# Keys and values of three context tiles made before the experts and kept in DRAM, in a two-layer perceiver kernel

## What is computed

```python
x = x + L0_xattn(layernorm(x), ctx_1024)      # 16 heads of 64
x = x + L0_attn(layernorm(x))                 # latent attention with rope ("mla")
x = x + L0_ffn(layernorm(x))                  # attention, then top-2 of 8 experts
x = x + L1_xattn(layernorm(x), ctx_1024, mask)# 16 heads of 16: the second cross-attention
x = x + L1_attn(layernorm(x))                 # causal attention
x = x + L1_ffn(layernorm(x))                  # weights of +1 and -1
# of L1_xattn, what matters here:
q = (query @ Wq + bq); k = (key @ Wk + bk); v = (value @ Wv + bv)
attn = softmax(where(mask == 0, -inf, q k^T * 16**-0.5));  out = (attn v) @ Wo + bo
```

## Time and profile before

| | us |
|---|---|
| median of 3 runs | 1094.91 |
| lowest, highest | 1089.47, 1100.26 |
| run that was profiled | 1091.17 |
| its span, first to last instruction | 1089.4 |

### The profile page before, as it was taken

The page is one execution under the profiler, slowest core; times in us unless marked ns, Lnnn a source line. Parts: engine busy times, 40 slices in busy tenths (PEclk is TensorE's granted clock), DMA queues, the critical chain, the costliest instruction groups (busy, mean ns, idle before and its releaser), DMA issues.

```text
span 1089.4 us, 27524 instructions
## 1 busy us (share of the span) xinstructions
PE 1025.6 (94%) x11715; PEld 883.0 (81%) x11715; DVE 640.2 (59%) x1376; ACT 472.3 (43%) x866; POOL 242.8 (22%) x381
## 2 busy tenths in 40 slices
PE   5999999999999899999399999997999998999998
PEld 4788888888888678887399999995888877887887
DVE  5745645545333455775659999976577652355342
ACT  3333333333333755643156677751534332464231
POOL 2311211211111124343414343414201000011000
PEclk9999999999999999997589999997999997999999
DMA  9300000000000800220226577613110001000000
GB/s 312 106 17 20 10 12 20 2 1 1 2 1 2 339 2 3 79 99 12 69 60 233 193 235 277 214 31 96 41 41 22 3 2 59 13 2 2 1 20 19
DMA packets 55672, 72.79 MB, mean 67 GB/s; under 512 B 8504, under 2 KB 48896, under 8 KB 54912
## 3 DMA queue, kind: packets, MB, share of 16 engines
q1 hardware_dynamic: 54016, 66.85, 18.4%
q0 software_dynamic: 1536, 4.20, 1.2%
HBM read 60.02 MB, written 11.01 MB: 65 GB/s over the span
## 4 chain that ended last, share of the span: by engine, by line
PE 84%; DVE 7%; ACT 3%; issue 3%; POOL 2%; DMA 1%; DVEq 0%; POOLq 0%; ACTq 0%
PE ps L615 8%; PE ps L630 8%; PE ps L2171 7%; PE ps L2187 7%; PE ps L2527 5%; PE ps L1469 4%; PE ps L599 3%; PE ps L1117 3%; PE ps L647 3%; PE ps L1387 3%; PE ps L667 3%; PE ps L569 3%; PE ps L1486 2%; PE ps L1426 2%; PE ps L1052 2%
## 5 line engine op out<-in xcount | busy, mean ns | idle before, releaser
L371 POOL TENSOR_TENSOR rn_tmp<-rn_cur,eps 128x1 f32<-128x1 f32 x48 | 14.6, 304 | 432.1 <-DVE rn_cur L365 432.0
L750 ACT ACTIVATE x0pT<-ps 128x512 f32<-128x512 f32 x64 | 38.3, 598 | 123.7 <-PE ps L630 123.7
L2171 PE MATMUL ps<-moe_xT_hi,ew_1hi 128*128 128x256 f32 x240 | 69.8, 291 | 2.3 <-DVE moe_xT_lo L2317 2.3
L2187 PE MATMUL ps<-ew_2hi,eh_hi 128*128 128x256 f32 x240 | 69.4, 289 | 2.4 <-DVE eh_lo L2325 2.4
L2323 DVE CAST eh_hi<-eh 128x512 fp32r<-128x512 f32 x60 | 63.4, 1056 | 13.9 <-ACT eh L2233 13.9
L2171 PE MATMUL ps<-moe_xT_lo,ew_1hi 128*128 128x256 f32 x240 | 68.9, 287 | 0.0
L2171 PE MATMUL ps<-moe_xT_hi,ew_1lo 128*128 128x256 f32 x240 | 68.8, 287 | 0.0
L2187 PE MATMUL ps<-ew_2hi,eh_lo 128*128 128x256 f32 x240 | 67.1, 279 | 0.0
L2187 PE MATMUL ps<-ew_2lo,eh_hi 128*128 128x256 f32 x240 | 66.9, 279 | 0.0
L857 DVE TENSOR_TENSOR x0A_lo<-ps,x0A_hi 128x512 fp32r<-128x512 f32 x64 | 41.0, 685 | 35.6 <-ACT x0A_hi L741 35.6
L2527 PE MATMUL ps<-f,ffw 128*128 128x512 f32 x256 | 59.2, 391 | 0.2 <-DVE f L2500 0.2
(11 more groups left out here) (330 smaller groups left out, 2832.1 us busy)
## 6 DMA issues: line engine op xcount, KB each, us to landing
ew<-L_ffn_W_dram SPq DMA_DIRECT2D x30, 1024.0 KB, 7.2
x0cin<-ctx_dram SPq DMA_DIRECT2D x8, 512.0 KB, 4.1
x1cin<-ctx_dram SPq DMA_DIRECT2D x8, 512.0 KB, 4.4
xg<-moe_in SPq DMA_DIRECT2D x15, 256.0 KB, 7.7
moe_out<-moe_y SPq DMA_DIRECT2D x15, 256.0 KB, 7.8
moe_in<-padneg SPq DMA_DIRECT2D x3, 1024.0 KB, 13.2
maskrow<-mask_BxS_ik_dram SPq DMA_DIRECT2D x2, 1024.0 KB, 7.7
x0wk<-L_xattn_Wkv_dram SPq DMA_DIRECT2D x1, 1024.0 KB, 7.1
```

The lines of the kernel that those rows point to most:

```text
L750: nc.scalar.activation(g.pT[:, u, :], ps[:, S_BANK[u % 2], :], ACT.Exp, scale=64.0 ** -0.5).then_inc(C0.exp, 1)
L2171: last = nc.tensor.matmul(ps[:, n % 3, j * BT:j * BT + BT], w[b % 2][:, i, f * P:f * P + P], v[b % 2][:, i, :], start=(i == 0 and m == 0), ...
L2187: last = nc.tensor.matmul(ps[:, O_BANK[b % 2] + c, 0:D], v[n % 3][:, j * BT + c * P:j * BT + c * P + P], w[b % 2][:, f, :], start=(f == 0 ...
```

## The change

With `EARLY` = 3, the K/V work of context tiles 0, 1 and 2 moves out of the second cross-attention.

- It is made in iterations 13 to 18 of the self-attention loop, between the pieces of the last items, on PE, ACT and DVE (`x1_cT`, `x1_k`, `x1_v`). Its buffers (`XE`) lie where the second expert's split weights and other late buffers stand, so the loads of those buffers and some splits come later.
- SP stores each finished tile (keys and values, 8.7 KB in each of 128 partitions, 1.1 MB) to the DRAM tensor `kv_early`, two buffers for three tiles, and loads all six parts again in and after the last expert block, into five buffers for keys and five for values.
- The split of the K/V weights is made twice, the first time in items 8 and 9, in place of two splits of expert 1, which move into expert block 0 (ACT, DVE and POOL one each for the parts 2 and 3).
- `weights_of(3)` moves behind `rows_of(2)`, into block 0. The load of `w_sq[1]` (1 MB) moves from the start of the kernel to block 5.
- In the second cross-attention tile 3's K/V work stands at the head, and the remaining four tiles are spread over the seven steps by `KV_STEP`: steps 0, 2, 4 hold a tile's `cT` and `k`, steps 1, 3, 5 its `v`, step 6 all of the last tile.
- `pool_x1` gathers two tiles before the first `rstd` where it gathered four; the others follow one for each norm.

```diff
+        EARLY = 3
...
+        class XE:
+
+            cin = nc.alloc_sbuf_tensor_at("xe_cin", [P, 2, 4, D], F32, offset=expert_at(1))
+            w_hi, w_lo = (nc.alloc_sbuf_tensor_at("xe_w_" + n, [P, KD, 2, D], F32R, offset=w_sq_at + 4 * KD * 4 * D + 4 * KD * 2 * D * i) for i, n in enumerate(("hi", "lo")))
+            cT_hi, cT_lo = (nc.alloc_sbuf_tensor_at("xe_cT_" + n, [P, KD, 512], F32R, offset=expert_at(7) + 4 * KD * 512 * i) for i, n in enumerate(("hi", "lo")))
+            kv = [nc.alloc_sbuf_tensor_at(f"xe_kv{i}", [P, KV_WORDS], F32, offset=expert_at(11) + 4 * KV_WORDS * i) for i in range(2)]
+            kT = [k[:, 0:KD * 512].rearrange("p (k n) -> p k n", k=KD) for k in kv]
...
+        KV_STEP = ((4, "k"), (4, "v"), (5, "k"), (5, "v"), (6, "k"), (6, "v"), (7, "kv"))
...
+        def wait_stored(eng, t):
+
+            if 1 < t < EARLY:
+                eng.wait_ge(C1.early_stored[t - 2], 16)
+
+        def wait_all_stored(eng):
+            for t in range(EARLY):
+                eng.wait_ge(C1.early_stored[t], 16)
+
...
-                fill_k(0, 0)
-                fill_k(0, 1)
-                fill_v(0, 0)
-                fill_v(0, 1)
+                fill_k(EARLY, 0)
+                fill_k(EARLY, 1)
+                fill_v(EARLY, 0)
+                fill_v(EARLY, 1)
                 fill_lat(0)
                 fill_q(0)
                 for t in range(T - 1):
                     old = t > 0
+                    j, part = KV_STEP[t]
                     scores(t, 0)
                     if old:
                         fill_pv(t - 1, 0)
-                    fill_cT(t + 1, 0)
-                    fill_cT(t + 1, 1)
+                    if part == "v":
+                        fill_v(j, 0)
+                    else:
+                        fill_cT(j, 0)
+                        fill_cT(j, 1)
                     if old:
                         fill_pv(t - 1, 1)
                     scores(t, 1)
                     if old:
                         fill_T(t - 1)
                     fill_lat(t + 1)
-                    fill_k(t + 1, 0)
+                    if part == "v":
+                        fill_v(j, 1)
+                    else:
+                        fill_k(j, 0)
                     if old:
                         fill_y(t - 1)
                     fill_neg(t, 1)
                     exponents(t, 0)
-                    fill_k(t + 1, 1)
+                    if part != "v":
+                        fill_k(j, 1)
                     fill_q(t + 1)
                     exponents(t, 1)
-                    fill_v(t + 1, 0)
-                    fill_v(t + 1, 1)
+                    if part == "kv":
+                        fill_v(j, 0)
+                        fill_v(j, 1)
                 return scores, fill_pv, fill_neg, fill_T, exponents, fill_y
 
...
         def pool_x1(pool):
-            for t in range(4):
+            for t in range(2):
                 moe_collect(pool, t)
             for phase, t in X1_ROWS:
                 row_rstd(pool, t, X1_ROWS[phase, t] % 2, phase, X1_ROWS[phase, t])
-                if phase == "x1" and t + 4 < T:
-                    moe_collect(pool, t + 4)
+                if phase == "x1" and t + 2 < T:
...
+                if span == 0 and n >= hi - 3:
+                    i = n - hi + 3
+                    if ahead:
+                        scores(n + 1)
+                    if front:
+                        fill_qk(n + 2, "k")
+                    elif i == 1:
+                        x1_k(0, 0)
+                    elif i == 2:
+                        x1_v(0, 1)
+                    elif i == 3:
+                        x1_k(1, 0)
+                    if back:
+                        fill_pv(n - 1, 0)
+                    if front:
+                        fill_qk(n + 2, "q")
+                    elif i == 1:
+                        x1_k(0, 1)
+                    elif i == 3:
+                        x1_k(1, 1)
+                    if back:
+                        fill_pv(n - 1, 1)
+                    if routed(span, n - 3):
+                        fill_router(n - 3)
+                    if front:
+                        fill_v(n + 2)
+                    elif i == 1:
+                        x1_v(0, 0)
+                    elif i == 3:
+                        x1_v(1, 0)
+                    elif i == 4:
+                        x1_k(2, 0)
+                        x1_k(2, 1)
+                    elif i == 5:
+                        x1_v(2, 1)
+                    if back:
+                        fill_T(n - 1)
+                    if here:
+                        exponents(n)
+                    if back:
+                        fill_y(n - 1)
+                    if i in (0, 2):
+                        x1_cT(i // 2, 0)
+                        x1_cT(i // 2, 1)
+                    if routed(span, n - 2):
+                        fill_mT(n - 2)
+                    if i == 3:
+                        x1_v(1, 1)
+                    if routed(span, n - 3):
+                        fill_rank(n - 3)
+                    if i == 3:
+                        x1_cT(2, 0)
+                        x1_cT(2, 1)
+                    elif i == 4:
+                        x1_v(2, 0)
...
+                    x1_v(2)
+                if span == 0 and 2 <= n < 8:
                     expert_upper(act, (n - 2) // 4, (n - 2) % 4)
+                if span == 0 and n == 8:
+                    act.wait_ge(ld["xw"], 64)
+                    nc.scalar.activation(XE.w_hi[:, :, :, :], xw[:, :, 1:3, :], ACT.Copy).then_inc(C1.w_hi, 1)
...
+            elif b == 1 and i > 1:
+                R1.wait_filled(act, EARLY - 1, "v1")
...
+            wait_all_stored(dve)
...
-                if p == 0 and 0 < b < NB - 1:
+                if p == 0 and b < NB - 1:
                     expert_lower(dve, b + 1, 2)
...
-            for i, w in enumerate("QKVO"):
-                whole(w_sq[1][:, :, i, :], weight("L1_attn_W_" + w), ld["sq1"])
...
+            def early_part(t, part):
+                at_kv = KD * 512 * part
+                dst = X1.v[t][:, :, :, :].rearrange("p k h d -> p (k h d)") if part else X1.kT[t][:, :, :].rearrange("p k n -> p (k n)")
+                sp.dma_start(dst, kv_dram[P * t:P * t + P, at_kv:at_kv + (KV_WORDS - KD * 512 if part else KD * 512)]).then_inc(ld_kv[t], 16)
 
...
+            def early_context(t):
+                sp.dma_start(XE.cin[:, t % 2, :, :], y_at[bass.ds(t, 1), :, :, :].rearrange("o p k d -> p (o k) d")).then_inc(ld_early[t % 2], 16)
+
+            def early_store(t):
+                for k in ("k0", "k1", "v0", "v1"):
+                    R1.wait_emptied(sp, t, k)
+                sp.dma_start(kv_dram[P * t:P * t + P, :], XE.kv[t % 2][:, :]).then_inc(C1.early_stored[t], 16)
+
             weights_of(2)
-            weights_of(3)
+
+            sp.wait_ge(MO.w_hi, 6)
+            sp.wait_ge(MO.w_lo_dve, 3)
+            sp.wait_ge(MO.w_lo_pool, 3)
+            early_context(0)
+            early_context(1)
+            R1.wait_filled(sp, 0, "cT1")
+            early_context(2)
+            sp.wait_ge(C1.early_ones, 1)
+            early_store(0)
+            early_store(1)
+            early_store(2)
             sp.wait_ge(MO.spread, 16 * 2 * T)
             rows_of(0)
+            wait_all_stored(sp)
             rows_of(1)
             rows_of(2)
...
+                if b == 0:
+                    weights_of(3)
                 if b + 3 < NB:
                     rows_of(b + 3)
+                if b == NB - 1:
+
+                    sp.wait_ge(MO.w_hi, 4 * (NB - 1))
+                    sp.wait_ge(MO.w_lo_dve, 2 * (NB - 1))
+                    sp.wait_ge(MO.w_lo_pool, 2 * (NB - 1))
+                    sp.wait_ge(MO.h_ps, NP * (NB - 1))
+                    early_part(0, 0)
+                    sp.wait_ge(MO.o_ps, NP * (NB - 1))
+                    early_part(0, 1)
                 if b > 0:
                     sp.wait_ge(MO.y_sb, b)
                     sp.dma_start(block_rows(moe_out, b - 1), ysb[(b - 1) % 2][:, :, :]).then_inc(y_stored[(b - 1) % 2], 16)
                     weights_of(b + 4)
                 if b in (6, 7):
                     sp.wait_ge(MO.pad, 2)
-                    ctx_tile(1, b - 6, b - 6)
+                    ctx_tile(1, EARLY + b - 6, (EARLY + b - 6) % 2)
+                if b == 5:
+                    R1.wait_filled(sp, EARLY - 1, "v1")
+                    for i, w in enumerate("QKVO"):
+                        whole(w_sq[1][:, :, i, :], weight("L1_attn_W_" + w), ld["sq1"])
+            for t in range(1, EARLY):
+                for part in range(2):
+                    early_part(t, part)
...
+            for i in range(2):
+                last = nc.gpsimd.memset(XE.v[i][:, :, :, 16:XVW], 1.0)
+            last.then_inc(C1.early_ones, 1)
```

(41 more changed lines are left out.)

202 lines of the change are left out of this document (139 added, 63 removed).

## The result

The change makes the kernel slower: 1135.73 us, median of 4 runs (1132.16 to 1141.12), against 1092.41 us before (1089.47 to 1100.26), a ratio of 1.0409 with a 95% interval of 1.0369 to 1.0449. The forecast was 1097 us. The profiled execution after has a span of 1130.4 us, 41.0 more than the 1089.4 before. In two of the runs further down some executions took over 1.5% longer than the fastest of the same kernel (two of four in the second run with small products, two of seven in the last run), and the ratios leave these out.

A forecast was written before the change was run, and what follows sets the result against it. PE's queue sets the end almost everywhere; +8 + 0.5 - 3.6 - 1.0 + 1.8 - 3.1 = +2.6 us on the profiled 1091.2 gives 1093.8, and the median lies 3.7 above: 1097. Range 1084 to 1110.

The forecast's parts named there:

- the stretch before the experts: Tail of the items before the experts: K/V work landing there makes the last rank later, +8 us (+4 to +12).
- hand-over: From last rank to first expert block: tile 2's store and the last scatters share DMA engines, +0.5 us (0 to +3).
- norm earlier, clock at the start: Second cross-attention's start: fewer gathers free POOL for the norm, -3.6 us; shorter idle keeps the clock up, -1.0.
- last store behind the loads: Before the second cross-attention: loads of tiles 1 and 2 delay the last store, gathers wait for it, +1.8 us.
- steps: Second cross-attention steps without three tiles' K/V work: of 21.2 us taken out, 3.1 us come back.
- The own case: Likeliest case, chance 0.4: the sum of the terms holds, clock stays up in the new steps; range 1090 to 1104.
- The rival: Clock falls within the new second cross-attention steps, some 6 us each, one or two falls: 1103 to 1109; chance 0.25.
- The rule weighed in the prediction: Trainium skill's section blaming idle PE between bursts for clock falls; by it gaps this short would leave the clock alone.
- the fall at 504.5: Tail before the experts: clock falls to 1.2 GHz though PE was busy 3.98 of the 4 us before.
- Steps bound by PE: Rival in the second cross-attention: all 21.2 us less come through, 1079; chance 0.12, including an unseen gain of that size.
- A tail that hides the work: Rival before the experts: idle PE and low-clock waste are filled in full, leaving +4 there: 1093; chance 0.13.
- Transfers that collide: Rival: last store waits out 2.2 MB and tile 2's store delays first rows, +6 over the sum, 1103; chance 0.1.

The follow-up runs named there:

- the second run with small products: Changed kernel plus 20 and 34 small unread products in PE's waits before second exponents and next scores; ratio 1.0495, runs from 1137 to 1158 us.
- the last run: Kernel before with two gathers fewer ahead of the first norm, plus extra wide products in the tail of the items; 1082.56 us, ratio 0.9917.
- the run with two gathers fewer: Kernel before with two gathers instead of four ahead of the first norm, the others each behind a norm; 1086.93 us, ratio 0.9976.
- the run with three wide products: Changed kernel plus three unread 128x512 products before the next tile's scores in steps 0 to 5; 1092.88 us, ratio 1.0030.
- the first run with small products: Changed kernel plus 36 and 62 small unread products in PE's waits before second exponents and next scores; 1200.12 us, ratio 1.1006.

## Why the prediction was wrong, point by point

**The time.** 1135.7 lies above the range of 1084 to 1110. Term by term:

| term | forecast | shown |
|---|---|---|
| the stretch before the experts | +8 (4 to 12) | +11.2 |
| hand-over | +0.5 | +0.7: the first rows are loaded 14.8 us later, the last rank is 14.1 later |
| norm earlier, clock at the start | -3.6 - 1.0 | -4.6, in the run with two gathers fewer |
| last store behind the loads | +1.8 | +2.5: from store to first gather 5.1 us for 2.6 |
| steps | -3.1 | -3.5 with three wide products in the wait; +33.3 in the changed kernel |

**The step that failed** is the choice of the likeliest case. The own case (0.4) let the clock stay up in the new steps, with the words that in the steady steps 1.2 us of scores and 2 us of values follow one another at a clock of 1.00. It did not: the clock fell at the start of six of the seven steps, and all seven took 167.0 us where the forecast had 130.6. That row was read rightly and carried over wrongly: in those steps v0 and v1 stood ahead of the scores. The change takes them away and puts 2.2 us and more of idle in their place, between the exponents, which are small, and the scores and values, which are small too. The rival said just that, and its mechanism is the one found.

**The rival's price.** It took 6 us a fall, and one or two falls. Against the run with three wide products, steps 1 to 5 and 6 are 28.2 and 7.5 us longer in the changed kernel: 35.7 us. Of these 4.1 are ACT's late starts (waits of 3.2, 4.4 and 3.2 us for 2.2); 31.6 are left for six falls, 5.3 each on the average and between 3 and 8. The price was near and the count was wrong. The steps are periodic: the gap that brings one fall comes back in each, and between two of them the clock recovers. By its own argument the rival was 6 x 6 = 36 us over the sum, 1133.

**What held.** Of 21.2 us taken out of the steps, hardly anything comes back, since the chain of scores, maximum, exponents and exponentials becomes the bound. The forecast steps were 18.2 us with K and 18.7 with V; at a full clock they took 18.12 and 18.65. The gathers' -4.6 us is met to a tenth. From the last rank to the first scores the terms shown add up to -1.4 us and the trace has -0.6; where the other 0.8 us are was not followed. With the clock held, the changed kernel is at 1092.9, nearer to the kernel before than the forecast of 1097; in part that is luck, since its profile (span 1090.8) has not the chance fall behind the last tile's scores, 5.7 us, which that of the kernel before has. (Three sums of the prediction are off by little: 3 x 7.1 is 21.3 and not 21.2, 3 x 0.2 + 2 x 0.7 is 2.0 and not 2.1, and 1093.8 + 3.7 is 1097.5.)

**The stretch before the experts.** The mechanism was right (the wide work keeps the clock up: 0.97 for 0.70), and the size off by 3.4 us. By the ledger of the windows shown, work at full clock grew by 21.9 us (forecast 21.2), the clock gave back 7.9 (9.4, all of it), idle went down by 2.9 (4.0).

**The rule weighed in the prediction.** The clock fell with PE busy for all of the 8 us before (806 to 814 in the first run with small products). In the prediction's own row, the 4 us before the fall at 504.5, the weighted values are 2.04 us; scores and the router, small products too, fill the rest. The Trainium skill, TensorE: Matmul & The Clock Gate, section HAM oscillation — how this bites in real kernels, describes such a fall in every turn of a loop and puts it down to PE idling for transfers between bursts; this case's traces agree that it repeats, here in six of seven turns, but the idle time is a wait of 2.2 to 4.4 us for ACT and for no transfer, and idle time is not needed for a fall.

**The other rivals.** Steps bound by PE (0.12): did not come, even at the full clock. A tail that hides the work: did not come. Transfers that collide: 0.9 us more than in the sum, hand-over and last store together.

## What to carry to other kernels

Wide matmuls that lie in another chain's waits did two things here: they used PE, and they held its clock. Before moving them out of a loop, look at what is left around each wait; if only small products stand on both sides, cost a fall of the clock in every turn, not one (here six in seven steps). If they must go, a few wide products in the wait, where they lengthen nothing, are worth trying first: here 0.7 us a step brought the time from 1136 to 1093 us, some 4 us of it by the late starts that went away with them.

## What was not expected of the hardware

- The clock fell without idle PE, and stayed up with some: it fell after 8.00 us of busy PE with mostly small products, and stayed at 1.00 with 1.2 to 1.4 us of idle once or twice in a step when 0.7 us of wide products stood in the wait.
- A fall may come or not in code that is the same: at 358 us in 4 of 14 profiles (2.9 us), some 21 us behind the last tile's first scores in 7 of 14 (5.7 us). A difference of one such fall between two single profiles says nothing about a change.
- Beside POOL's indirect gathers other engines start late without a releaser in the profile: ACT by 1.0 to 2.3 us, PE by 0.4 us twice, steps 1.3 us longer. With the gathers moved off the end of the exponents ACT's late starts are gone; which gathers do it is open.
- A product of 128x512 in fp32 took 0.9 us, in fp32r 0.24 us.
